# Mixing each batch by itself and adding the two parts of y on their way through DRAM

## What is computed

```python
W = weights[condition]
y = jnp.einsum('bct,bcd->bdt', x, W)
gate_logits = jnp.einsum('bsd,ed->bse', y, gate_w)
weights, selected = jax.lax.top_k(gate_logits, 2)        # softmax over the two
result = jnp.einsum('bsd,od->bso', y, base_w) + base_b
low = jnp.einsum('bsd,erd->ebsr', y, lora_A)
lora_out = jnp.einsum('ebsr,eor,bse->bso', low, lora_B, w_full)
return x + result + 2.0 * lora_out
```

## Time and profile before

| | us |
|---|---|
| median of 3 runs | 478.52 (478.49 to 480.21) |
| profiled execution, its own time | 478.04 |
| its span, first to last instruction | 476.3 |
| PE busy | 469.9 |
| DVE busy | 351.2 |
| ACT busy | 159.5 |
| POOL busy | 117.0 |

### The profile page before, as it was taken

One profiled execution on the slowest core, in us unless ns is written; L12 is line 12 of the kernel. 1 busy time (PEld: TensorE's weight loads), 2 busy tenths in 40 slices (PEclk: granted clock), 3 DMA queues, 4 the chain that ended last, 5 costly groups with the idle time before them and its releaser, 6 DMA issues.

```text
span 476.3 us, 8144 instructions
## 1 busy us (share of the span) xinstructions
PE 469.9 (99%) x2660; PEld 460.7 (97%) x2660; DVE 351.2 (74%) x636; ACT 159.5 (33%) x262; POOL 117.0 (25%) x113
## 2 busy tenths in 40 slices
PE   8999999989999999999999999999999999999997
PEld 8999999989999999999999999999999999999996
DVE  4867979897686867869587686867869587585843
ACT  5734444223332422333223332322333223432300
POOL 2344241041420414123041420414114041310400
PEclk9999999999999999999999999999999999999999
DMA  8976633626355262743625356262643626343202
GB/s 314 411 226 223 194 95 132 217 72 223 112 183 194 96 227 54 246 128 132 220 88 199 110 179 195 88 221 65 231 144 133 212 87 210 112 170 120 89 22 88
DMA packets 49275, 76.91 MB, mean 161 GB/s; under 512 B 13666, under 2 KB 32226, under 8 KB 49250
## 3 DMA queue, kind: packets, MB, share of 16 engines
q1 hardware_dynamic: 37586, 71.88, 43.5%
q10 hardware_dynamic: 11664, 4.72, 3.8%
HBM read 41.98 MB, written 34.60 MB: 161 GB/s over the span
## 4 chain that ended last, share of the span: by engine, by line
PE 97%; DMA 1%; issue 0%; DVE 0%; ACT 0%; SPq 0%
PE acc L907 50%; PE acc L899 29%; PE acc L945 10%; PE mixed L939 9%; DMA x_sb<-in_x_first 1%; PE acc L925 0%; PE mixed L925 0%; DVE y_lo L611 0%; ACT y_hi L464 0%; DVE x_sb L892 0%; SPq L285 0%
## 5 line engine op out<-in xcount | busy, mean ns | idle before, releaser
L386 POOL TENSOR_TENSOR x_sb<-x_sb,bias 128x1024 f32<-128x1024 f32 x32 | 76.9, 2422 | 221.4 <-DVE x_sb L744 198.2
L899 PE MATMUL acc<-r_hi,y_lo 128*128 128x392 f32 x256 | 87.0, 340 | 0.2 <-DVE y_lo L611 0.2
L899 PE MATMUL acc<-r_hi,y_hi 128*128 128x392 f32 x256 | 86.9, 339 | 0.0
L899 PE MATMUL acc<-r_lo,y_hi 128*128 128x392 f32 x256 | 86.6, 339 | 0.0
L907 PE MATMUL acc<-t_hi,s_hi 128*128 128x384 f32 x224 | 74.9, 334 | 1.4 <-issue 1.4
L907 PE MATMUL acc<-t_lo,s_hi 128*128 128x384 f32 x224 | 74.9, 334 | 0.0
L907 PE MATMUL acc<-t_hi,s_lo 128*128 128x384 f32 x224 | 74.8, 334 | 0.0
L907 PE MATMUL acc<-t_lo,y_hi 128*128 128x384 f32 x216 | 72.4, 335 | 0.0
L907 PE MATMUL acc<-t_hi,y_lo 128*128 128x384 f32 x216 | 72.3, 335 | 0.0
L907 PE MATMUL acc<-t_hi,y_hi 128*128 128x384 f32 x216 | 72.2, 334 | 0.0
L652 DVE TENSOR_TENSOR y_lo<-y_turned,y_hi 128x512 fp32r<-128x512 f32 x60 | 45.2, 793 | 25.6 <-ACT y_hi L520 25.4
(11 more groups left out here) (81 smaller groups left out, 741.5 us busy)
## 6 DMA issues: line engine op xcount, KB each, us to landing
x_sb<-in_x SPq DMA_DIRECT2D x32, 512.0 KB, 4.7
out<-x_sb SPq DMA_DIRECT2D x31, 512.0 KB, 3.1
y_scratch<-y_whole SPq DMA_DIRECT2D x60, 256.0 KB, 2.1
y_moved<-y_scratch SPq DMA_DIRECT2D x120, 128.0 KB, 2.8
t_raw<-in_w_quads SPq DMA_DIRECT2D x4, 768.0 KB, 10.0
scratch<-low_turns ACTq DMA_DIRECT2D x16, 128.0 KB, 1.7
low_turns<-scratch ACTq DMA_DIRECT2D x64, 32.0 KB, 2.3
r_raw<-in_w_plain SPq DMA_DIRECT2D x8, 196.0 KB, 5.3
```

The costliest lines, as they stand in the source:

```text
L386: nc.gpsimd.tensor_tensor(x_sb[:, slot(c), :], x_sb[:, slot(c), :], bias[:, :], ALU.add) \
L899: return nc.tensor.matmul(acc[:, i, 0:NP], y_part[:, i, k, :], w_part[:, k, :], start=(k == 0 and product == 0), stop=(k == KT - 1 and pro ...
```

## The change

Every batch is mixed by itself, with all 128 rows of PE. The upper 64 partitions of the moving operand hold one part of x and the lower 64 the other (high in the batch's own half, low in the other half: x_parts gets a batch index, and `x_high` and `x_low` run once for each batch on 64 partitions). The weight matrix is W high beside W low, the same on both halves of the partitions; POOL makes it with one copy for each batch, and nothing needs to be zeroed. One matmul for each half of the columns gives, on partitions 0 to 63, W high × (x high + x low), and on 64 to 127, W low × (x high + x low). A pair takes four matmuls. The two results have to be added: SP writes partitions 0 to 63 to y_scratch, and POOL then issues a transfer of partitions 64 to 127 to the same place that adds to what is there (`sum_parts`). Ahead of it stands an addition of one column of the bias, token, which waits for the one before it. y_whole is doubled, one room for each batch, and `PITCH`, the row length of the r matrices in SBUF, goes from 448 to 416. The orders of PE, ACT and DVE are written anew around the halves.

The core of the diff:

```diff
             def move(j, u, i):
-                s = 3 * j + u
-                for h in range(2):
-                    sp.wait_ge(y_copied, 4 * s + 2 * i + h + 1)
-                    half = slice(h * (T // 2), (h + 1) * (T // 2))
-                    sp.dma_start(y_scratch[i, :, half], y_whole[:, half]).then_inc(y_out[h], 16)
+                n = 6 * j + 2 * u + i
+                for b in range(2):
+                    sp.wait_ge(y_copied, 4 * n + 2 * b + 2)
+                    sp.dma_start(y_scratch[i, batch(b), :], y_whole[0:CH, b, :]).then_inc(y_out[b], 16)
+                sp.wait_ge(y_sum, 32 * (n + 1))
                 for q in range(QUARTERS):
-                    if q % 2 == 0:
-                        sp.wait_ge(y_out[q // 2], 16 * (2 * s + i + 1))
...
+            def sum_parts(j, u, i):
+                n = 6 * j + 2 * u + i
+                for b in range(2):
+                    pool.wait_ge(y_out[b], 16 * (n + 1))
+                    if b == 1 and (u > 0 or i > 0):
+                        pool.wait_ge(turned, 2 * n)
+                    if u > 0 or i > 0 or b > 0:
+                        pool.wait_ge(token_ready, 2 * n + b)
+                    nc.gpsimd.tensor_tensor(token, bias[:, 0:1], bias[:, 1:2], ALU.add).then_inc(token_ready, 1)
+                    pool.dma_start(y_scratch[i, batch(b), :], y_whole[CH:P, b, :], accum_op=ALU.add) \
+                        .then_inc(y_sum, 16)
...
+            def y_copy(j, u, i, b):
+                n = 6 * j + 2 * u + i
+                if u > 0 or i > 0:
+                    act.wait_ge(y_sum, 32 * n)
+                    if u > 0:
+                        act.wait_ge(turned, 2 * n - 2)
                 for h in range(2):
-                    act.wait_ge(mix_done, 4 * s + 2 * i + h + 1)
...
+                    act.wait_ge(mix_done, 4 * n + 2 * b + h + 1)
+                    nc.scalar.copy(y_whole[:, b, h * (T // 2):(h + 1) * (T // 2)], mixed[:, h, :]).then_inc(y_copied, 1)
...
-            def mix(j, u, i):
+            def mix(j, u, i, b):
...
-                    for m, (w_part, x_part) in enumerate(((0, 0), (1, 0), (0, 1))):
-                        last = nc.tensor.matmul(mixed[:, h, :], w_sel[:, i, w_part, :],
-                                                x_parts[:, x_part, h * 512:(h + 1) * 512], start=(m == 0), stop=(m == 2))
-                    last.then_inc(mix_done, 1)
+                        pe.wait_ge(y_copied, 4 * n + 2 * b + h - 1)
+                    nc.tensor.matmul(mixed[:, h, :], w_sel[:, i, b, :], x_parts[:, b, h * 512:(h + 1) * 512],
+                                     start=True, stop=True).then_inc(mix_done, 1)
```

More of the change, by code:

```diff
@@ L208, in adaln_ffn_kernel @@
         y_copied = sem("y_copied")
-        y_out = [sem(f"y_out{h}") for h in range(2)]
+        y_out = [sem(f"y_out{b}") for b in range(2)]
+        y_sum = sem("y_sum")
+        token_ready = sem("token_ready")
         moved = [sem(f"moved{i}") for i in range(2)]
@@ L264, in slot, with batch @@
             return c % SLOTS
+        def batch(b):
+            return slice(b * CH, (b + 1) * CH)
         block = ctx.enter_context(nc.Block())
@@ L568, in step @@
                     t_high(2, T3)
+                if ahead:
+                    y_copy(j, u, 0, 1)
                 gate_exp(j, u)
+                if ahead:
+                    x_high(j, u, 1, 1)
                 if u == 1:
@@ L575, in step @@
                 if ahead:
-                    y_copy(j, u, 1)
+                    y_copy(j, u, 1, 0)
                 if u != 1:
                     turn_low_out(j, u)
+                if split:
+                    x_high(j, u, 2, 0)
+                if ahead:
+                    y_copy(j, u, 1, 1)
+                if split:
+                    x_high(j, u, 2, 1)
+                if u != 1:
+                    turn_low_in(j, u)
                 if ahead:
@@ L581, in step @@
                     y_high(j, u, 0, 1)
-                if u != 1:
-                    turn_low_in(j, u)
-                if split:
-                    x_high(j, u, 2)
                 lowT_high(j, u)
@@ L842, in step @@
                 if ahead:
-                    x_low(j, u, 1)
+                    x_low(j, u, 1, 0)
                 rank_gates(j, u)
                 take(j, u, 0, 1, 0, 0, BW)
+                if ahead:
+                    x_low(j, u, 1, 1)
                 apply_gates(j, u)
+                if u == 2:
+                    t_low(1, T1)
+                take(j, u, 1, 3, 0, BW, 2 * BW)
+                if split:
+                    x_low(j, u, 2, 0)
                 if ahead:
                     turn(j, u, 0)
-                if ahead and u > 2:
+                    take(j, u, 2, 5, 1, 0, 2 * BW)
+                if split:
+                    x_low(j, u, 2, 1)
+                if ahead:
                     y_low(j, u, 0, 0)
                     y_low(j, u, 0, 1)
-                take(j, u, 1, 3, 0, BW, 2 * BW)
-                if u == 2:
-                    y_low(j, u, 0, 0)
-                    y_low(j, u, 0, 1)
-                if u == 2:
-                    t_low(1, T1)
-                if split:
-                    x_low(j, u, 2)
-                if ahead:
-                    take(j, u, 2, 5, 1, 0, 2 * BW)
                     lowT_low(j, u)
+                    take(j, u, 3, 7, 0, BW, 2 * BW)
                 else:
@@ L1039, in step @@
                 if ahead:
-                    mix(j, u, 0)
+                    mix(j, u, 0, 0)
                 plain_pair(j, u, 1).then_inc(plain_done, 1)
+                if ahead:
+                    mix(j, u, 0, 1)
                 pe.wait_ge(res_ready, 2 * s)
@@ L1055, in step @@
                     return
+                mix(j, u, 1, 1)
                 if u == 2:
```

113 lines of the change are left out of this document (58 added, 55 removed).

## The result

The changed kernel takes 684.1 us (683.9 to 684.7, four runs); the kernel before takes 478.5 (477.7 to 480.2, four runs). The ratio is 1.431, with a 95% interval of 1.429 to 1.433. I had forecast 558, with 612 as the upper end: the direction was right, but the loss is 206 us where I said 80.

What follows compares the result with a forecast made beforehand. PE bound the old kernel; the change's loop through both accumulates would take 34.4 us a step, 5.7 over 28.69. Closing 14 times adds 80 us to 478, giving 558 us, range 508 to 612.

Steps and rivals of the forecast that it cites:

- first ring: One step's loop through both pairs' accumulates, the x load, DVE and ACT: 27.4 us + 2 D, 34.4 us; chance 0.72.
- second ring: Loop through PE, one accumulate and the x load: 28.0 us + D, 31.5; as rival, alone setting the step, 517, chance 0.10.
- copy of (1,0): ACT's copy of the second pair's first mixing result out of PSUM, claimed to wait for both accumulates of pair 0.
- copy of (1,1): ACT's copy of the second pair's second mixing result, claimed to stand behind x_high, which needs the first x load; 1.10 us.
- PE's 13.9 us: PE time saved by four mixing matmuls a pair instead of six; forecast to be no part of the sum, since PE waits.
- D: Time of one accumulate transfer issued by POOL into y_scratch: taken as 3.5 us, bounds 2.1 to 4.9.
- The writes: SP's transfers of partitions 0 to 63 to y_scratch, on both loops: 2.1 us each from issue to landing, bounded by 3.1.
- The load: First x load of a step, in SP's queue behind the y_moved transfers that wait for the sums: 4.0 us, between 3.4 and 4.7.
- The clock: Rival: PE's clock falls to 1.2 GHz after waits, for half of 13.9 us of PE work; total 615, chance 0.08.
- mix(1,1): PE's mixing of the second batch of a step's second pair, last of four mixings sharing the same two PSUM banks.
- the one in which nothing is late: Rival: the way of y has room to spare and PE stays the bound at 27.77 us a step; 464 us, chance 0.03.
- The range: Total time of 508 to 612 us around the forecast; the forecast's own bounds were 519 to 597.

Runs made afterwards that it cites:

- Kernels 1 and 2: Changed kernel with POOL's bias add cut to one column, 644.3 us; changed kernel with the full add issued ahead of the second pair's accumulates, 640.9 us.
- kernel 1: Changed kernel with POOL's bias add cut from 1024 columns to one, so the bias is left out of nearly all the result: 644.3 us.
- kernels 3 and 5: Changed kernel with SP's x loads issued ahead of the wait for the sums, 651.2 us; changed kernel with the accumulates not issued, 599.3 us.
- kernel 3: Changed kernel with SP's two x loads of a step issued ahead of the wait for the first pair's accumulates: 651.2 us.

## Why the prediction was right, and where it was wrong

- **Direction: right; which ring sets the step: wrong.** I had the first ring at 34.4 and the second at 31.5; measured, the first takes 39.3 and the second 43.8, so the second bound. The waits that I had built both on came: the loads behind the wait for the sums, the copy of (1,0) behind both accumulates, x_high ahead of the copy of (1,1): each is a wait of the trace, fourteen times. PE's 13.9 us count for nothing, as said. Moving the loads alone gave 33 us, and without accumulates 85. The four mixing matmuls took their 0.23 us where the clock was up, and the accumulates landed in 4.2.
- **The step that failed: the second ring.** I wrote that PE's last product follows the take and the low-rank part follows the product, 3.1 us. But the low-rank product also waits for the low-rank split, which stands on DVE behind x_low and both y_low. That way is 8.7 us, of which 3.9 would be there without a hindrance (0.92 + 1.22 + 1.29 + 0.50, from take to end of the split) and 4.8 is the block by the bias adds. The other branch, take and last product, was too short as well: 4.9 us for my 3.06, by the lower clock, so that of the 4.8 PE waited 3.8. Kernels 1 and 2 showed the block: 40 and 43 us, up to where the first ring took over. I had read POOL's adds only as work that must fit, and had moved nothing of POOL past DVE in my order; the earlier trace rows had the hint, y_low twice at 1.82 for 1.29.
- **First ring: right in its pieces, small in its terms.** 39.3 us for 34.4. D at 4.0 to 4.2 lay within my 2.1 to 4.9, in the upper half, for which I had named reasons. The writes at 2.9 lie by the bound that I had named (3.1) and not by the value that I took (2.1), and the additions with their hand-overs cost 0.6 to 1.1 each where I had charged a bare 0.1.
- **The load: mis-sized.** 4.0 for 4.8 to 5.3. I had taken a value between the least and the median of two loads, and already the least of after is 3.8 where it was 3.4. What lengthens them is not shown: in the step of kernel 1, with the same order on SP, the load took 4.8.
- **The clock: right as a rival, but it came together with the forecast,** not in place of it. The low-rank product at 0.50 takes 5.49 for 2.8, and the products behind mix(1,1), which are not on this ring, 7.86 for 6.2. I priced the clock as a case with a chance of 0.08, though waits of PE follow from every case but the one in which nothing is late. The Trainium skill's warning that the prediction cited (TensorE: Matmul & The Clock Gate, section Why this matters for your kernels) is borne out by the windows at 0.50.
- **The range** held one mechanism's bounds at a time. Even my own bounds for the first ring, taken together (D 4.9, load 4.7, both writes 3.1), give 597 + 10 + 28 = 635 and not 612. In the step above all the larger misses had one sign: 1.3 (load), 1.4 (write), 0.9 (addition and accumulate), 5.7 (DVE's way and block), 2.7 (clock). Their sum is 12.0 of the 12.4 us that I was short there.

## What to carry to other kernels

When a sum closes over a ring of several engines, walk each engine's own queue for every link: the product waits not only for its operand but for all that stands ahead of the operand's last step. A change that lets DVE's work bunch up moves it under POOL's two-input operations; ask of each long POOL operation what DVE will run beside it afterwards, not how busy POOL is. And once TensorE waits at all, charge the work behind each long wait at the lower clock as part of the forecast, not as a rival to it.

## What the runs showed of the hardware that I had not expected

- Two POOL adds of 2.4 us back to back kept one DVE subtraction with two SBUF inputs waiting for both of them in the kernel after (up to 5.70 us for 0.69); in kernels 3 and 5 two subtractions waited for one add each (at most 2.96 and 2.90). Before, the two transposes beside the same adds took 1.30 us (1.26 at 202.87, without an add beside them), and a take out of PSUM (215.23) 0.69.
- Accumulating in DRAM costs 1.2 us more than a plain write of 256 KB (4.1 against 2.9), when little else moves; beside two loads, a store and writes it took 7.7.
- The same 256 KB written from 64 partitions with 4 KB each took 2.9 to 3.2 us, from 128 with 2 KB each 2.1; beside moved loads 3.6 (kernel 3).
- Matmuls put into a wait did not help where 2.5 us of it stayed open behind them: after 26 of them the clock still read 0.50 for the next 4 us.
